# A post-norm decoder layer in fp32: the small fp32 products of a round gathered into four stretches, the start and the second matrix rearranged

## What is computed

```python
x = layernorm(x + self_attention(x))          # 8 heads, linear: no softmax between q, k and v
x = layernorm(x + cross_attention(x, ctx))    # 16 heads of 32, softmax over 154 keys, masked
x_prev = x shifted by one row
r = sigmoid((mu_r * x + (1 - mu_r) * x_prev) @ W_r.T)
k = square(relu((mu_k * x + (1 - mu_k) * x_prev) @ W_k.T))
x = layernorm(x + r * (k @ W_v.T))
```

## Time and profile before

| | us |
|---|---|
| median of 3 runs | 939.41 |
| lowest, highest | 938.14, 939.75 |
| the profiled execution | 940.32 |
| its span on the core | 938.2 |

### The profile page before, as it was taken

The page is one execution under the profiler, slowest core; times in us unless marked ns, Lnnn a source line. Parts: engine busy times, 40 slices in busy tenths (PEclk is TensorE's granted clock), DMA queues, the critical chain, the costliest instruction groups (busy, mean ns, idle before and its releaser), DMA issues.

```text
span 938.2 us, 18936 instructions
## 1 busy us (share of the span) xinstructions
PE 912.5 (97%) x6676; PEld 729.4 (78%) x6676; DVE 667.9 (71%) x1979; ACT 552.4 (59%) x1654; POOL 515.4 (55%) x507
## 2 busy tenths in 40 slices
PE   5999999998999999999999999999999999999997
PEld 5877657666788888887878787878787878787876
DVE  6487554556686877777777777777777777777775
ACT  6455305657675757575656575757575656666631
POOL 1034015657676666666566666675757584847421
PEclk9999999999999999999999999999999999999999
DMA  8593010102110101011100010010101010100001
GB/s 279 187 303 137 23 25 24 42 1 73 48 30 24 30 24 30 24 30 67 43 24 30 24 28 26 16 39 9 45 8 46 8 46 9 45 2 23 2 23 45
DMA packets 30872, 45.64 MB, mean 49 GB/s; under 512 B 2747, under 2 KB 15547, under 8 KB 30523
## 3 DMA queue, kind: packets, MB, share of 16 engines
q1 hardware_dynamic: 26123, 35.26, 11.7%
q10 hardware_dynamic: 4656, 9.18, 2.8%
HBM read 34.10 MB, written 9.70 MB: 47 GB/s over the span
## 4 chain that ended last, share of the span: by engine, by line
PE 77%; DVE 5%; issue 2%; ACT 2%; POOL 0%; POOLq 0%; DVEq 0%; ACTq 0%
PE dense L87 18%; PE dense L89 17%; PE dense L88 17%; PE turned L1450 6%; PE scores L1438 5%; PE rest_value L1464 4%; PE rest_value L1468 3%; PE dense L1350 2%; PE rest_value L1456 1%; PE turned L1350 1%; PE dense L1394 1%; PE scores L1356 1%; DVE mix_k_raw L1049 1%; DVE prob L1009 1%; ACT prob L744 1%
## 5 line engine op out<-in xcount | busy, mean ns | idle before, releaser
L1259 POOL TENSOR_TENSOR row_inv<-row_sum,minus_one 128x4 f32<-128x4 f32 x128 | 141.8, 1108 | 249.7 <-ACT prob L744 246.6
L744 ACT ACTIVATE prob<-prob,row_min 128x154 f32<-128x154 f32 x512 | 209.9, 418 | 16.8 <-DVE row_min L1009 16.8
L1265 POOL TENSOR_TENSOR prob<-prob,row_inv 128x512 f32<-128x512 f32 x128 | 147.0, 1148 | 0.0
L1009 DVE CUSTOM_DVE_ANT_0 prob<-scores,mask_add 128x154 f32<-128x154 f32 x512 | 129.3, 310 | 6.6 <-PE scores L1438 6.4
L752 ACT ACTIVATE prob_t<-turned 128x512 f32<-128x512 f32 x128 | 76.1, 595 | 61.8 <-PE turned L1450 60.5
L744 ACT ACTIVATION_READ_ACCUMULATOR prob<-prob,row_min 128x1 f32 x512 | 98.9, 193 | 0.0
L1016 DVE TENSOR_TENSOR o_t_lo<-rest_value,o_t_hi 128x256 fp32r<-128x256 f32 x64 | 26.9, 420 | 83.8 <-ACT o_t_hi L763 83.8
L1450 PE MATMUL turned<-ident,prob 128*128 128x128 f32 x512 | 79.4, 278 | 0.4 <-POOL prob L1265 0.4
L763 ACT ACTIVATE o_t_hi<-rest_value 128x256 fp32r<-128x256 f32 x64 | 24.5, 382 | 88.2 <-PE rest_value L1468 88.2
L87 PE MATMUL dense<-xt_hi,cross_wq_hi 128*128 128x256 f32 x256 | 74.2, 290 | 1.3 <-DVE xt_lo L1000 1.3
L87 PE MATMUL dense<-mix_k_hi,ffn_wk_hi 128*128 128x256 f32 x256 | 75.2, 294 | 0.0
(11 more groups left out here) (266 smaller groups left out, 2602.7 us busy)
## 6 DMA issues: line engine op xcount, KB each, us to landing
x_rows<-x_rows SPq DMA_DIRECT2D x32, 256.0 KB, 4.7
xt_raw<-x_cols SPq DMA_DIRECT2D x16, 512.0 KB, 3.7
out<-gate_then_y SPq DMA_DIRECT2D x15, 512.0 KB, 2.8
mask_in<-mask SPq DMA_DIRECT2D x16, 154.0 KB, 2.3
cross_wv<-cross_wv SPq DMA_DIRECT2D x1, 1024.0 KB, 9.1
cross_wk<-cross_wk SPq DMA_DIRECT2D x1, 1024.0 KB, 9.7
self_wv<-self_wv ACTq DMA_DIRECT2D x1, 1024.0 KB, 5.6
self_wk<-self_wk ACTq DMA_DIRECT2D x1, 1024.0 KB, 10.4
```

The costliest lines, as they stand in the source:

```text
L744: m = act.activation(keys, keys, ACT.Exp, bias=row_min[:, buf, t, h:h + 1], scale=-1.0, accum_out=row_sum[:, buf, t, h:h + 1])
L1009: m = dve.tensor_tensor_reduce(prob[buf][:, t, h * CTX:(h + 1) * CTX], s_bank[:, h, t * CTX:(t + 1) * CTX], mask_add[n % 2][:, t, :], -SCA ...
L1259: pool.tensor_tensor(row_inv[:, buf, t, :], row_sum[:, buf, t, :], minus_one[:], ALU.pow).then_inc(*p_inv.up)
L1265: pool.tensor_tensor(keys[:, :, 0:P], keys[:, :, 0:P], inv.broadcast_to([P, HPG, P]), ALU.mult).then_inc(*p_norm.up)
```

## The change

- **Start.** SP issues the loads of x tiles 4 to 7 ahead of cross_wv and cross_wk. ACT, DVE and PE treat eight tiles before the context products (PE: six before). ACT splits tiles 8 to 11 ahead of the key copies.
- **Rounds on PE.** The order becomes K O O Y | T Tr S T v | Y R R | T Tr X S X X2 v X2 T | K Q Q | T Tr S T v | V V | T Tr S T v. The scores of the next group's second quarter and its first transposes move into this round's end. Before, each quarter's blocks stood one or two at a time between the dense products.
- **Banks.** d0 and d1 are taken in turn along the round, and since a round has 15 turns, an odd number, every product changes its bank with the round. The second half of x2's transposes goes to a dense bank. Waits follow.
- **ACT, DVE and POOL** are reordered to match. In round 0 the four copies `take_u` come together, ahead of `x_high(1)` (before, `x_high` came first), and PE makes `fold_u(0, 1, 2, 3)`, `y_product(1, 0)` and `y_product(1, 1)` in a row.
- **Second matrix.** m_hi and m_lo are made in four pieces each, at the end of round 6 on ACT and DVE.

```diff
             sp.dma_start(ctx_t[:], wide("ctx_cols")).then_inc(*ctx_in.up)
+            for j in range(RING, 2 * RING):
+                load(j)
             sp.dma_start(w_v[:], wide("cross_wv")).then_inc(*wv_in.up)
-            load(RING)
-            load(RING + 1)
             sp.dma_start(w_k[:], wide("cross_wk")).then_inc(*wk_in.up)
             sp.dma_start(bv_row[:], io["rows"][3:4, :].broadcast_to([P, D])).then_inc(*bv_in.up)
             sp.dma_start(col_sb[:], io["cols"]).then_inc(*cols_in.up)
-            for j in range(RING + 2, 5 * RING):
+            for j in range(2 * RING, 5 * RING):
...
-            high(0, 1, 2, 3)
+            high(0, 1, 2, 3, 4)
             part_high(0)
-            high(4)
+            high(5, 6, 7)
             part_high(1)
-            high(5)
             part_high(2)
-            high(6, 7)
             load_square("self_wv")
...
+            high(8, 9, 10, 11)
...
-            high(*range(8, 14))
+            high(12, 13)
...
-            sums(0, 1, 2, 3, 4, 5)
+            sums(*range(2 * RING))
...
-        two = {"y": (d1, d0), "x1": (d1, d0), "q": (d0, d1), "o": (d1, d0), "x2": (t_bank, t_bank), "k": (d0, d1), "r": (d1, d0),
-               "v": (d0, d1)}
+        dense = d0, d1
+        place_in_round = {"k": (0, 10), "o": (1, 2), "y": (3, 4), "r": (5, 6), "x1": (7, 8), "x2": (9, 9), "q": (11, 12),
+                          "v": (13, 14)}
...
+        def bank(kind, n, i):
+            if (kind, n) in last:
+                return last[kind, n][i]
+            if kind == "x2" and i == 0:
+                return t_bank
+            return dense[(n + round_of[kind] + place_in_round[kind][i]) % 2]
...
+            def next_m_high():
+                act.wait_ge(*m_here.at(0))
+                for k in range(KT):
+                    act.activation(m_hi[:, k, :], m_raw[:, k, :], ACT.Copy).then_inc(*m_hi_ok.up)
...
             for n in range(-1, LAST):
...
+                if live(n):
+                    take_turned(n, 0, 0)
+                if n == 0:
+                    take_u(0, 1, 2, 3)
                 if a:
                 if a:
                     x_high(a)
+                if live(n):
+                    exponentials(n, 1, 0)
...
-                if a == GPB - 1:
-                    act.wait_ge(*m_here.at(0))
-                    act.activation(m_hi[:], m_raw[:], ACT.Copy).then_inc(*m_hi_ok.up)
...
                 exponentials(a, 0, 0)
+                exponentials(a, 0, 1)
+                if a == GPB - 1:
+                    next_m_high()
...
+            def next_m_low():
+                for k in range(KT):
+                    dve.wait_ge(*m_hi_ok.at(0, k + 1))
+                    dve.tensor_tensor(m_lo[:, k, :], m_raw[:, k, :], f32(m_hi[:, k, :]), ALU.subtract).then_inc(*m_lo_ok.up)
...
+                if live(n):
+                    weigh(n, 3, 1)
                 if live(f):
                     r_mix_low(f)
-                if live(n):
-                    weigh(n, 3, 1)
...
             for n in range(-1, LAST):
                 a, f, e = n + 1, n - 1, n - 2
                 if live(e):
                     k_product(e, 0)
                 if n == 0:
                     fold_kv()
-                if live(n):
                     scores(n, 1)
                     transposes(n, 0, 0)
-                if n == 0:
-                    fold_u(0, 1)
+                    fold_u(0, 1, 2, 3)
                 if live(f):
                     o_product(f, 0)
-                if live(n):
-                    transposes(n, 0, 1)
-                if n == 0:
-                    fold_u(2, 3)
-                if live(f):
                     o_product(f, 1)
                 y_product(a, 0)
-                if live(n):
-                    values(n, 0)
+                if n == 0:
+                    y_product(a, 1)
+                if live(n):
+                    transposes(n, 0, 1)
                     scores(n, 2)
                     transposes(n, 1, 0)
-                y_product(a, 1)
+                    values(n, 0)
+                if n:
+                    y_product(a, 1)
                 if n == -1:
                     fold_t(1, 2)
-                if live(n):
-                    transposes(n, 1, 1)
                 if n == 1:
                     fold_m(2)
                 if live(e):
                     r_product(e, 0)
                     r_product(e, 1)
+                if live(n):
+                    transposes(n, 1, 1)
+                x1_turn(a, 0)
+                if live(n):
+                    scores(n, 3)
+                x1_turn(a, 1)
                 if live(f):
                     x2_turn(f, 0)
                 if live(n):
                     values(n, 1)
-                x1_turn(a, 0)
                 if live(f):
                     x2_turn(f, 1)
                 if live(n):
-                    scores(n, 3)
-                x1_turn(a, 1)
+                    transposes(n, 2, 0)
                 if n == -1:
                     fold_t(3)
-                if live(n):
-                    transposes(n, 2, 0)
                 if n == 0:
                     fold_c()
                 if live(e):
                     k_product(e, 1)
+                q_product(a, 0)
+                q_product(a, 1)
+                if live(n):
                     transposes(n, 2, 1)
-                    q_product(a, 0)
-                else:
-                    q_product(a, 0)
-                    if live(n):
-                        transposes(n, 2, 1)
-                q_product(a, 1)
-                if live(n):
+                scores(a, 0)
+                if live(n):
+                    transposes(n, 3, 0)
                     values(n, 2)
-                scores(a, 0)
-                if live(n):
-                    transposes(n, 3, 0)
                 if n == 0:
                     fold_m(0)
+                    fold_m(1)
                 if n == 1:
                     fold_m(3)
                 if live(e):
                     v_product(e, 0)
+                    v_product(e, 1)
                 if live(n):
                     transposes(n, 3, 1)
-                if n == 0:
-                    fold_m(1)
-                if live(e):
-                    v_product(e, 1)
-                if live(n):
+                    scores(a, 1)
+                    transposes(a, 0, 0)
                     values(n, 3)
 
 
```

More of the change, by code:

```diff
@@ L343, in dve_program @@
                                   ALU.add).then_inc(*v_sum.up)
-            low(*range(8, 18))
+            low(*range(10, 18))
             take_sums(0)
@@ L490, in pe_program @@
                 m.then_inc(*k_mm.up)
-            sums(*range(6, HALF + 2))
+            sums(*range(2 * RING, HALF + 2))
             pe.wait_ge(*zeroed.at(0))
@@ L1162, in dve_program @@
                     take_t(3)
+                if live(n):
+                    masked_min(n, 3, 0)
+                    o_low(n, 1)
+                    masked_min(n, 3, 1)
+                if n == 0:
+                    take_c()
                 if live(f):
@@ L1178, in dve_program @@
                     k_mix_low(f)
+                masked_min(a, 0, 0)
                 if live(n):
                     o_low(n, 2)
-                if a == GPB - 1:
-                    dve.wait_ge(*m_hi_ok.at(0))
-                    dve.tensor_tensor(m_lo[:], m_raw[:], f32(m_hi[:]), ALU.subtract).then_inc(*m_lo_ok.up)
-                masked_min(a, 0, 0)
                 masked_min(a, 0, 1)
```

131 lines of the change are left out of this document (58 added, 73 removed).

## The result

| | before | after |
|---|---|---|
| median, us | 939.19 | 953.62 |
| lowest, highest | 938.14, 939.75 | 953.12, 955.48 |
| span of the profiled execution | 938.2 | 951.3 |

The ratio is 1.0159, with a 95% interval of 1.0141 to 1.0176: the changed kernel is slower by 14.4 us. The forecast was 945.2, 6 us slower than before. The sign is right and the time lies within the range, but the loss is more than twice as large.

What follows compares the result with a forecast made beforehand. PE was taken to bound the kernel, busy for 97% of the span. Steady rounds +5.3, start -5.6, second matrix -3.2 and round 0 +9.3 sum to +5.8 us: 946.1 profiled, 945.2 as median, range 936 to 957.

Steps and rivals of the forecast that it cites:

- The start: Before the context product: eight tiles without a break, product starting between 18.8 and 23.9, taken as 19.7; gain 5.6 us.
- Round 0: PE idles 4.2 us ahead of y and 4.7 ahead of x1's transposes, clock falls twice; loss 9.3 us.
- The second matrix: Round 6 and behind it: the 1.88 us wait and 1.3 us of low clock go; gain 3.2 us.
- The steady round: Rounds 1 to 14: eight tiled entries instead of six, 0.38 us more a round, 5.3 us in all; no new waits.
- three closest meeting points: Steady round: a quarter's second transposes after ACT's copy, scores to group a's transposes, quarter 2's copy behind the k mix; each fits.
- The first rival: Steady round: a wait at the copy behind the k mix, 0.7 us a round, 955 us; chance 0.15.
- Values to scores is free: PE's tiled blocks: a value product takes 1.00 us ahead of scores or a dense product, so this change costs nothing.
- An entry costs 0.09 us: PE's tiled blocks: going from transposes into scores, or from a dense matmul into a value product, adds 0.09 us.
- From dense to transposes and back costs nothing: Between k and q products: six transposes take 0.66 us, 0.11 each, so the change is free, fp32r or fp32.
- By number format: Rival: PE pays for changes between fp32 and fp32r, not tilings; 13.3 us less over 14 rounds, 926.6 us; chance 0.07.
- No holes in round 0: Rival: POOL and DVE get through sooner, round 0 costs 2 us instead of 9.3, 937.9 us; chance 0.21.
- The clock behind the longest stretch without a dense product: Rival: 4.8 us without a dense product lowers the clock each round, 1.3 us each, sum +24, 963 us; chance 0.05.

Runs made afterwards that it cites:

- repaired round 0: The changed kernel with x_high(1) first on ACT, y_finish(1, 1) ahead of masked_min(0, 2, 0) on DVE, scale(1, 1) ahead of weigh(0, 2, 0) on POOL: 943.14 us.
- alternating run: The kernel before with values(n, 0) and scores(n, 2) cut in halves and alternated, two more changes of tiling a round: 944.37 us, ratio 1.0062.
- moved block: The kernel before with values(n, 0) moved from ahead of scores(n, 2) to behind transposes(n, 1, 0) in each round: 943.58 us, ratio 1.0061.

## Why the prediction was right in sign and wrong in size

**The start.** Forecast -5.6, measured -4.8. The SP queue issued cross_wv at 8.73 (forecast 8.9), the context product started at 20.66 (19.7), within the bounds given. The lower bound adds up to 18.7, not 18.8, which changes nothing, since PE is not through before 18.98. Right.

**Round 0.** Forecast +9.3, measured +9.0. Both holes stood where the walk along the queues had put them, at 4.10 and 4.44 us against 4.2 and 4.7, released by POOL's xt_lo and DVE's x, and the clock fell twice. The repaired round 0 gave back 10.5 us in the time. One wait, of 1.08 us for ACT's prob_t at 166.89, was not in the walk; it stands ahead of the second hole, which waited for POOL and DVE. This was the surest part, since nearly every step of it had a duration in a row of before.

**The second matrix.** Forecast -3.2, measured -2.3. The named wait and the low clock went, as forecast. But the 1.3 us for the clock were there to win back in some executions only: behind the same wait it fell in two traces of seven. That the trace of before was one of them is luck. The step that failed is "PE has 5.6 us of v product before it": that covers ACT and PE, but DVE was not free in time, and o and y waited.

**The steady round: the term that failed.** Forecast 5.3 us over rounds 1 to 14; measured, the rows of the table from group 1 on give 0.7 + 3.1 + 5.8 + 0.8, and 0.8 in the round of the second matrix, 11.2. These 5.9 us are most of the 7.3 by which the spans differ more than forecast (13.1 against 5.8); the start adds 0.8, the second matrix 0.9, and round 0 takes off 0.3. The rest of the 14.4 lies between profiled executions and medians. Two steps failed.

First, "I take 0 for new waits". The text named three closest meeting points and missed the one that closed: y_product(a, 0) against `o_finish(f, 0)`. DVE in before:

```profile
529.00 1.00 DVE L985 TENSOR_SCALAR gate_then_y<-gate_then_y,moments,rstd 128x512 f32<-128x512 f32 x2
529.92 0.68 DVE L1022 TENSOR_TENSOR x<-dense,x 128x512 f32<-128x512 f32 x1
```

It ended that step 8.7 us into the round (529.92 and 0.68, from 521.86), and y began at 10.5. After, it ended 8.6 us into the round, and y was ready at 8.5. So DVE came at the same time as before, while PE had got there 1.9 us sooner, because scores and transposes that stood ahead of y had moved behind it. That DVE came no sooner is the norm's two halves in part: 1.72 us after (536.84), 1.00 in before. At 1.00, by my estimate, o_finish(f, 0) would have ended 0.7 us earlier, and y would not have waited. The first rival, a wait in each steady round, was right in kind, and wrong in place and size (0.33 us a round instead of 0.7). By the prediction's own last sentence, a wait in each round makes it wrong.

Second, the prices of the changes: 0.49 us a round measured, 0.38 forecast. The count of six and eight entries was right. Three prices were not.

- *Values to scores is free.* A value block takes 1.00 us ahead of scores and ahead of a dense product. But both cases end with a change, and before has no value block with another behind it; the 1.00 holds the fixed part in both. The alternating run shows it.
- *An entry costs 0.09 us.* That was read behind a dense product and behind x's transposes. Six of the eight entries of the new order come from transposes of the probabilities or the rest, and cost 0.17 to 0.18. At 0.09 these transposes would have grown by 0.54 us a round; they grew by 1.12, from 3.89 to 5.01.
- *From dense to transposes and back costs nothing.* The 0.66 us for six transposes held 0.08 that belongs to the first dense matmul behind them: the q product starts at 506.37, so the six take 0.58. In before nine stretches of dense products a round begin behind a small block, in the new order four. The forecast's prices make the dense products 0.16 us a round shorter (two more ways out of v, four entries fewer); they got 0.66 shorter, from 34.82 to 34.16, read without the wait at y.

So two errors of half a microsecond a round, of opposite sign, left 0.11 between them. That 0.38 came so near to 0.49 is luck. The Trainium skill's rule, which I had weighed against the 1.00 us, does not shrink the sum either: if every change of the tiling costs, the count goes from 14 to 16.

**The other rivals.** By number format: wrong as the whole price, since the moved block cost 0.23 us without a further change of format, and the round got longer, not shorter. But what it was built on is there: a way back from plain fp32 transposes to an fp32r product costs 0.08 us, and the gathering saves some. Whether the format or something else about the transposes sets that price was not tested. No holes in round 0: out. The clock behind the longest stretch without a dense product: it did not fall in the steady rounds:

```profile
500.00:860.00 360.00, 359.45 (x2810) 293.37 (x2810) 269.17 (x844) 224.51 (x721) 235.19 (x224) 1.00 0.08 25
```

What stays open is why transposes of the probabilities cost twice as much as x's ahead of a tiled block.

## What to carry to other kernels

Count the borders between tilings along the matmul queue, and take their mean price from two kernels whose counts differ; a block that is never seen without a border behind it says nothing on what the border costs. Then price each border from a row with the same two neighbours: an entry cost 0.09 us behind one kind of block and 0.17 behind another here. And a price of nothing needs the same care as any other: a cost on the first matmul of the next product hides in what looks like the length of the block before. When blocks are gathered, list for every product that moves to an earlier time in the round who last reads its bank, and where that reader stands now: each small block taken out from in front of a product was cover for a reader. Read steady rounds from start to start over a whole round, since a wait shorter than the modelled length of the matmul before it is marked nowhere.

## What the runs showed that I had not expected

A direct change between row tiles and column tiles costs 0.18 us (alternating run), within the 0.16 to 0.25 us of changes from and to the whole array. The same wait of about 1.9 us left the clock at 1.00 in five traces and was followed by 1.2 GHz in two. A wait of 0.25 us cost 0.32, since the matmul behind it takes 0.30 to the next start instead of 0.23. The same subtraction of 128 x 512 on DVE took 0.68 and 0.66 us in two places and 2.87 in another (the second piece in the row of 3.47), and the norm's two halves 1.00 us in before and 1.72 after (529.00 and 536.84), 1.27 of it in the first. In both slow cases an instruction of POOL ran at the time, and the slow one ended 0.55 and 0.3 us behind it: xt_lo from 473.51 to 475.93 us, the slow piece until 476.5; the weighing of the probabilities from 536.33 to 537.83, the slow half until 538.1. That this is the cause was not tested by itself.
